# Paired context attention in a new order, v swaps issued by ScalarE, and a context fetch moved behind a self attention

## The reference

```python
x = x + _L0_xattn_ref(_layernorm(x), ctx_512, ...)   # causal self attention + context attention, 16 heads, with MLPs
x = x + _L0_attn_ref(_layernorm(x), ...)             # self attention, 16 heads of 16, rotary
x = x + _L0_ffn_ref(_layernorm(x), ...)              # 8 experts of 352, top 2, and a shared one
x = x + _L1_xattn_ref(_layernorm(x), ctx_512, ctx_512, ...)   # context attention with one head
...                                                  # recurrence, experts; L2: context attention, rotary attention, experts
x = x + _L3_xattn_ref(_layernorm(x), ctx_512, ...)   # context attention, 16 heads of 16, 1601 keys
x = x + _L3_attn_ref(_layernorm(x), ...)             # self attention, 16 heads of 16, with biases
x = x + _L3_ffn_ref(_layernorm(x), ...)              # 16 experts of 128 and a shared one
```

## Time and profile before

| | |
|---|---|
| median of 3 runs | 2265.95 us (2257.9 to 2266.71) |
| profiled execution | 2265.01 us, of which span 2263.2 us |
| PE busy | 2018.8 us, 89% of the span |
| DVE, ACT, POOL busy | 62%, 50%, 26% |
| mean granted TensorE clock | 0.945 of full |
| third context attention | 1698 to 2083 us of the span |
| self attentions | a1 54 to 92 us, l0a 661 to 692, l2a 1544 to 1565, l3a 2121 to 2147 |
| first experts (l0f) | from 715 us |

### The profile page before, as it was taken

One profiled execution on the slowest core, in us unless ns is written; L12 is line 12 of the kernel. 1 busy time (PEld: TensorE's weight loads), 2 busy tenths in 40 slices (PEclk: granted clock), 3 DMA queues, 4 the chain that ended last, 5 costly groups with the idle time before them and its releaser, 6 DMA issues. The chain is left out here.

```text
span 2263.2 us, 42827 instructions
## 1 busy us (share of the span) xinstructions
PE 2018.8 (89%) x14978; PEld 1739.0 (77%) x14978; DVE 1392.2 (62%) x2718; ACT 1141.2 (50%) x2324; POOL 595.6 (26%) x536
## 2 busy tenths in 40 slices
PE   5877999999887998589899999988888998998898
PEld 2766999999566885278699999966767888887677
DVE  8455777777355443831577777745456777776466
ACT  3235666666423432321566666633446676665254
POOL 2323212221012330200322222102325555440034
PEclk9798999999996998689999999999998999999899
DMA  5252101000041213431110110002226555551022
GB/s 217 58 233 103 42 31 46 30 30 0 36 149 58 79 54 138 191 133 64 59 46 31 36 39 30 0 0 84 80 71 164 152 138 139 139 132 42 19 79 76
DMA packets 49603, 183.66 MB, mean 81 GB/s; under 512 B 9392, under 2 KB 14896, under 8 KB 46128
## 3 DMA queue, kind: packets, MB, share of 16 engines
q1 hardware_dynamic: 49456, 181.75, 25.0%
HBM read 125.72 MB, written 13.90 MB: 62 GB/s over the span
## 5 line engine op out<-in xcount | busy, mean ns | idle before, releaser
L616 PE MATMUL ps<-pTh,ch 128*128 128x256 f32 (+1 forms) x1248 | 382.3, 306 | 26.2 <-DVE pTl L1491 25.0
L1026 ACT ACTIVATE pTh<-ps 128x512 fp32r<-128x512 f32 (+1 forms) x512 | 235.8, 519 | 258.0 <-PE ps L926 257.7
L617 PE MATMUL ps<-pTl,ch 128*128 128x256 f32 (+1 forms) x1248 | 350.2, 281 | 0.0
L618 PE MATMUL ps<-pTh,cl 128*128 128x256 f32 (+1 forms) x1248 | 349.9, 280 | 0.0
L1084 DVE TENSOR_TENSOR pTl<-ps,pTh 128x512 fp32r<-128x512 f32 (+1 forms) x512 | 277.3, 583 | 83.8 <-ACT pTh L1026 83.2
L616 PEld LDWEIGHTS ps<-pTh,ch 128*128 128x128 f32 (+1 forms) x1248 | 236.1, 189 | 43.0 <-DVE pTl L1491 32.4
L617 PEld LDWEIGHTS ps<-pTl,ch 128*128 128x128 f32 (+1 forms) x1248 | 236.9, 190 | 0.0
L618 PEld LDWEIGHTS ps<-pTh,cl 128*128 128x128 f32 (+1 forms) x1248 | 235.9, 189 | 0.0
L616 PE MATMUL ps<-cTh,qh 128*128 128x512 f32 (+2 forms) x512 | 184.8, 361 | 16.7 <-POOL ql L880 11.9
L618 PE MATMUL ps<-cTh,ql 128*128 128x512 f32 (+2 forms) x512 | 179.9, 351 | 0.0
L617 PE MATMUL ps<-cTl,qh 128*128 128x512 f32 (+2 forms) x512 | 179.5, 351 | 0.0
(11 more groups left out here) (406 smaller groups left out, 4613.2 us busy)
## 6 DMA issues: line engine op xcount, KB each, us to landing
stacked<-weights SPq DMA_DIRECT2D x168, 100.2 KB, 2.2
stacked<-weights SPq DMA_DIRECT2D x168, 100.0 KB, 2.2
w<-l1f_w_in SPq DMA_DIRECT2D x16, 1024.0 KB, 8.2
wg<-l0f_guide_in SPq DMA_DIRECT2D x10, 704.0 KB, 5.2
z<-ctx_in SPq DMA_DIRECT2D x8, 832.0 KB, 12.8
z<-z SPq DMA_DIRECT2D x8, 832.0 KB, 10.0
keys<-ctx_in SPq DMA_DIRECT2D x8, 832.0 KB, 10.7
zT<-zT SPq DMA_DIRECT2D x8, 801.0 KB, 9.1
```

Of the source, the lines that this page charges most:

```text
L616: pe.matmul(out, high, moving_high, start=start, stop=False)
L617: pe.matmul(out, high, moving_low, start=False, stop=False)
L618: return pe.matmul(out, low, moving_high, start=False, stop=stop)
L1026: nc.scalar.activation(pTh[0:w, PARTS[g][0]:PARTS[g][0] + n, slot, :], ps[0:w, turned_bank[slot][g], 0:n * P].rearrange("p (k r) -> p k r" ...
```

## The change

There are three parts.

**Order of the third context attention.** Key tiles 0 and 1 get banks of their own (4 and 5) and are made right after the first half of the scores of slot 0; the second half follows behind them. The turned groups get other banks, and another order: 1, 0, 2, 3 for slot 0 and 0, 1, 3, 2 for slot 1. ACT copies the key tiles second and third in the couple, and puts copies of turned groups between the two halves of the exponents. DVE takes the two maxima apart and subtracts between them. SP's and POOL's streams stay as they are, and so do the waits of `keep_key` and of `move`.

**Swaps.** The two DMAs from v to v are issued by ACT, as soon as the last part of v is copied: in `dense` the values are now the first four products, all copied by ACT, and the DMAs stand behind the fourth; in `rotary_projections` they stand behind the fourth copy of v, ahead of the copies of the turned rows of the tile before. ACT waits for its own copies and for POOL's column of ones first.

**Fetch.** `context.fetch` of pairs 0 and 1 stands behind `inner_attention("l0a")`, ahead of `gated_experts("l0f")`.

```diff
@@ dense: behind ACT's copy of product n @@
+                            if n == NT - 1 and taken_first is not None:
+                                scalar.wait_ge(taken_by_scalar, NT)
+                                taken_first(nc.scalar)
...
@@ self_attention @@
+        def swap_halves(engine, v, swapped):
+
+            engine.dma_start(v[0:S, :, 1], v[S:P, :, 0]).then_inc(swapped, 16)
+            engine.dma_start(v[S:P, :, 1], v[0:S, :, 0]).then_inc(swapped, 16)
...
-                    @block.sync
-                    def _(sp):
-                        sp.dma_start(v[0:S, :, 1], v[S:P, :, 0]).then_inc(swapped, 16)
-                        sp.dma_start(v[S:P, :, 1], v[0:S, :, 0]).then_inc(swapped, 16)
...
@@ paired_attention @@
-                turned_bank = (4, 5, 7, 4), (5, 7, 4, 5)
+                turned_bank = (7, 4, 5, 4), (7, 4, 7, 5)
+                turn_place, low_place = ((2, 1, 3, 4), (1, 2, 4, 3)), ((2, 1, 4, 3), (1, 2, 4, 3))
+                key_bank = 4, 5
...
@@ paired_attention, PE, steady couple @@
-                                pe.wait_ge(probs_half, v)
-                                turn_second(0, v - 1)
-                                scores(u, step, first)
+                                first_scores(u, step, first)
+                                pe.wait_ge(low_kept, 4 * v - 6)
+                                turn(0, v - 1, 1)
...
-                                turn_second(1, v - 1)
-                                turn_second(2, v - 1)
+                                pe.wait_ge(low_kept, 4 * v - 5)
+                                key_tile(u, step, 0, final)
+                                pe.wait_ge(low_kept, 4 * v - 4)
+                                key_tile(u, step, 1, final)
+                                second_scores(u, step, first)
+                                key_bank_free(u, step, 0, final)
+                                turn(1, v - 1, 1)
+                                key_bank_free(u, step, 1, final)
+                                turn(3, v - 1, 1)
+                                pe.wait_ge(low_kept, 4 * v - 3)
+                                turn(2, v - 1, 1)
                                 values(0, c - 1, i, first and u == 2, new_batch)
-                                turn_second(3, v - 1)
                                 values(1, c - 1, i)
-                                if key_tiles(u // PER, (u // 2) % 4, final):
-                                    pe.wait_ge(low_kept, 4 * v - 2)
-                                key_tile(u, step, 0, final)
-                                scores(u + 1, step, first)
-                                turn_first(0, v)
-                                turn_first(1, v)
-                                key_tile(u, step, 1, final)
+                                first_scores(u + 1, step, first)
+                                second_scores(u + 1, step, first)
+                                turn(1, v, 0)
+                                pe.wait_ge(low_kept, 4 * v)
+                                turn(0, v, 0)
+                                turn(2, v, 0)
                                 values(2, c - 1, i)
-                                key_bank_free(u, step, final)
-                                turn_first(2, v)
                                 values(3, c - 1, i)
-                                turn_first(3, v)
+                                pe.wait_ge(low_kept, 4 * v + 1)
+                                turn(3, v, 0)
...
@@ paired_attention, ACT @@
                                     keep(0, v - 1, 1)
+                                    for chunk, tile, j in tiles:
+                                        keep_key(step, first, i, at, tile, j)
                                     keep(1, v - 1, 1)
+                                    keep(3, v - 1, 1)
+                                exponents(v, 0, first and u < 2, 0)
+                                if before:
                                     keep(2, v - 1, 1)
-                                exponents(v, 0, first and u < 2, 0)
                                 exponents(v, 0, first and u < 2, 1)
-                                if before:
-                                    keep(3, v - 1, 1)
-                                    for chunk, tile, j in tiles[0:1]:
-                                        keep_key(step, first, i, at, tile, j)
+                                keep(1, v, 0, c if before else None)
                                 keep(0, v, 0, c if before else None)
-                                keep(1, v, 0, c if before else None)
-                                if before:
-                                    for chunk, tile, j in tiles[1:]:
-                                        keep_key(step, first, i, at, tile, j)
                                 exponents(v + 1, 1, first and u < 2, 0)
-                                exponents(v + 1, 1, first and u < 2, 1)
                                 keep(2, v, 0, c if before else None)
                                 keep(3, v, 0, c if before else None)
+                                exponents(v + 1, 1, first and u < 2, 1)
...
@@ paired_attention, DVE @@
+                                first_maximum(v, 0)
                                 if before:
                                     low(0, v - 1, 1)
-                                maximum(v, 0)
+                                second_maximum(v, 0)
                                 if before:
                                     low(1, v - 1, 1)
+                                    low(3, v - 1, 1)
                                     low(2, v - 1, 1)
-                                    low(3, v - 1, 1)
-                                maximum(v + 1, 1)
+                                first_maximum(v + 1, 1)
+                                second_maximum(v + 1, 1)
+                                low(1, v, 0)
                                 low(0, v, 0)
-                                low(1, v, 0)
                                 if before:
                                     store(c - 1, 2 * step + (u - 2) // PER, ((u - 2) // 2) % 4)
+                                low(3, v, 0)
                                 low(2, v, 0)
-                                low(3, v, 0)
...
@@ rotary_projections, ACT @@
                             keep_values(t)
+                            if t == NT - 1:
+                                act.wait_ge(values_kept, NT)
+                                act.wait_ge(counted, NT)
+                                swap_halves(nc.scalar, v, swapped)
                             keep_turned(t - 1)
...
@@ perceiver_kernel @@
-            context.fetch(nc.sync, 0)
-            context.fetch(nc.sync, 1)
             gains = weights("l0a")
             with expert_weights("l0f", 352) as held:
                 inner_attention("l0a", True, True, "bo", xn, mid,
                                 [(mid, inner, (), (gains("gamma"), gains("beta"))), (x, xn, (inner,), None)],
                                 held.split_first)
+                context.fetch(nc.sync, 0)
+                context.fetch(nc.sync, 1)
                 gated_experts("l0f", 8, 10, 352, "pair", held)
```

## The result

The changed kernel takes 2322.49 us (median of 4 runs, 2311.82 to 2325.07) beside 2261.93 for the kernel before (4 runs, 2256.58 to 2266.71); the ratio is 1.0259, with an interval from 1.0216 to 1.0303. Forecast were 2333 us and a range of 2292 to 2352. The profiled execution has a span of 2323.3 us and a mean granted clock of 0.932, where the earlier trace rows and the table ahead of them came from one of 2263.2 us and 0.945.

The account below looks back on a forecast made before the run. PE was taken as the bound, busy 344.4 of 385 us in the third context attention; 2265.0 + 54 (order, waits, clock) - 6 (swaps) + 19 (fetch) = 2332, stated as 2333 us against the median, range 2292 to 2352.

Parts of the forecast that it names:

- The new order by itself: Third context attention: shorter couples without the new wait, -33 us, between -40 and -15.
- The couple was laid out at 10.35 us: Third context attention: tightest loop of the new couple, through DVE, 10.35 us against 11.57 before.
- The wait of the key copy: Third context attention: ACT waits 4.8 us for key tile 0's moves, PE stalls 4.7, 13 times, +61 us.
- The landing at X + 9.9: Third context attention: all twelve key-move DMAs land 9.9 us after X, the end of issue of the previous unit's scores.
- X + 5.1: Third context attention: ACT wants key tile 0 5.1 us after issue of the previous unit's scores ends (X).
- The lower clock: Third context attention: PE at the 1.2 GHz level behind each stall, 2.0 us, 13 times, +26 us.
- the stage's clock at 0.85: Third context attention: granted clock of the whole stage falls from 0.98 to about 0.85.
- The expert's weights: Experts of layer 0: expert 1's guide weights land behind the moved fetch, PE stalls 17.2 us, +19 with lower clock.
- the chain from the landing to PE: Experts of layer 0: PE goes on 4.1 us after the guide weights land, as in the second experts.
- The swaps: Self attentions: sum of -6 us, with -7 in l0a and 0.5 for each block where ACT pays for issues.
- the 7 us of l0a: Layer 0's late self attention: PE's 2.36 us swap wait goes and clock partly rises, -7 us (-2 to -10).
- the reading in the prediction: Swaps: another issuer saves only the time to issue, so swaps alone bring 0 to -1 us, the rest the fetch's.

Follow-up runs that it names:

- order_busy: Kernel before with the new attention order alone, plus 34 PE products during each of the 13 key-copy waits: 2286.37 us, ratio 1.0126.
- swaps_only: Kernel before with only the swaps of v issued by ACT and the values first in dense: 2261.54 us, ratio 0.9987.
- order_only: Kernel before with only the new order of the third context attention: 2309.66 us beside 2265.59, ratio 1.0191.
- second_room_only: Kernel before, old order, with only a second place for the key rows and their high part: 2265.00 us beside 2260.81, ratio 1.0008.
- order_second_room: Kernel before with the new order and a second place for the key rows and their high part: 2235.31 us beside 2265.59, ratio 0.9876.

## Why the prediction was right

**The new order by itself: -33 forecast, -29 found in the first trace, -23 to -32 over all.** The couple was laid out at 10.35 us and is 10.36 to 10.42. The missing 4 us are not couples but, by their size, batches: the wait for POOL's low part of the transposed context, 5.3 us in four, was nowhere in my layout; the traces of the kernel before and of the changed one don't have it.

**The wait of the key copy: 4.7 for PE each, 13 times, +61 forecast; 4.27 each and 55.5 in sum found.** The landing at X + 9.9 was exact in the couple shown, and so was the moment at which ACT wants it (X + 5.1). The mean is lower because waits differ (4.15 to 5.08 in the first six of the changed kernel) and SP's 24 issues took 15.1 to 16.6 us instead of the 16.36 that I took for all. The term was 6 us too large, the largest error of the sum.

**The lower clock: 2.0 for each wait, +26 forecast; 1.9 and 24.4 found.** I drew it from one row of another stage, and `order_busy` bears it out, within the wide interval given there. I had the stage's clock at 0.85, and it is 0.90: a couple with the wait has 0.80, one without 1.00, and the first and last batches have few waits or none.

**The expert's weights: +19 forecast, 17.1 found** at the first product of expert 1 (746.44 against 729.32), of which 14.57 is the wait and 2.5 the lower clock. They landed at 737.0 and not at 739.7, as 8.07 MB took 21.7 us. The 23.7 us of the earlier trace rows for 7.81 MB are no rate: by the DMA view that stretch runs at 400 to 443 GB/s in the middle too, but at 210 or less from 664.3 us on. The other half of the mechanism, that the chain from the landing to PE takes 4.1, was 4.2 (737.01 to 741.21).

**The swaps: -6 forecast; alone -8 to +2 measured.** The sign is not settled. I gave the 7 us of l0a to parts 2 and 3 together. By the landings they are the fetch's: the swap issued 4.2 us earlier by ACT landed no sooner while the fetch was ahead. This bears out the reading in the prediction by which the swaps alone bring 0 to -1, as far as l0a goes. In the changed kernel l0a takes 27.1 us, 4.1 less and not 7. In a1, where I had put nothing, the changed kernel ends 2.7 us later than its start's offset. From its first scores to the mark behind it a1 takes 52.4 to 53.6 us in the five kernels with the new order of `dense`, and 49.2 to 52.6 in the nine without, so that a term of 1 to 2 us is likely, and was missing.

The terms of the stage sum to +48.4 where I had +54, the experts to +17.7 where I had +19, the rest to -6.0 (60.1 - 48.4 - 17.7) where I had -6. The last agreement is luck: the rest is +4.1 up to the mark l0a_in, -4.0 from there to the experts, -1.7 between the marks l1f_in and `ctxT_in`, and -4.4 behind the third context attention, of which -4.6 stand in l3a and are not the change's, as the last section shows.

## What to carry to other kernels

When a copy is moved earlier in a loop, look not only at what it waits for now but at how much earlier than its other waits it would come: a transfer that lands 1.2 us ahead of its reader shows no wait, and is 4.8 us late once the reader comes 6 us sooner. A fetch moved off a busy moment lands on the next one, and costs where something small and urgent stands behind it in the queue; put it behind that. When a wait vanishes, look whether the transfer landed sooner or its reader came later: here the swap issued 4.2 us earlier landed at 669.4 instead of 668.7. And price a stall of PE at its length and then the slower products behind it, here 1.9 us for each.

## What the runs showed of the hardware

The same code of one stage can take two lengths in executions of kernels that differ elsewhere. The 586 matmuls of the last self attention (l3a), windows view, in the kernel before, in `swaps_only`, in the changed kernel, in `order_only` and in `second_room_only`:

```profile
2120.68:2147.22 26.54, 22.37 (x586) 20.11 (x586) 12.79 (x20) 8.01 (x18) 2.01 (x2) 0.74 0.10 24
```

```profile
2115.80:2142.07 26.27, 22.09 (x586) 19.84 (x586) 12.78 (x20) 8.01 (x18) 2.01 (x2) 0.74 0.01 3
```

```profile
2185.55:2207.44 21.89, 17.18 (x586) 15.08 (x586) 12.78 (x20) 7.79 (x18) 2.01 (x2) 1.00 0.02 4
```

```profile
2168.88:2190.77 21.89, 17.17 (x585) 15.09 (x586) 12.78 (x20) 7.78 (x18) 2.01 (x2) 1.00 0.12 29
```

```profile
2119.40:2141.29 21.89, 17.17 (x585) 15.08 (x586) 12.78 (x20) 7.79 (x18) 2.01 (x2) 1.00 0.12 29
```

`swaps_only` and the changed kernel have the new swaps, and differ by 4.4 us; `order_only` and `second_room_only` have the old ones, and take the short length, while the kernel before, with the same code of this stage, takes the long one. Over all traces the nine kernels with the old code take 21.9 us three times, 24.3 once and 26.3 to 27.4 five times, and the five with the new code 21.9 three times, 22.8 and 26.3. What differs in all pairs is the granted clock, 0.74 or 1.00, and DVE's busy time is the same to 0.01. So a stage in which PE waits 0.8 to 1.0 us at a time, as this one does in the kernel before, can run at either level, and 4 to 5 us of a single profile's difference there say nothing about the change. In l0a the same code has both lengths too (31.2 us in the kernel before, 23.7 in `order_second_room`), but there the level goes along with the wait for the swap, as the table above shows. What decides which level a stage gets was not tried.
